# Two DMA queues instead of one for the count stage of a graph network kernel

## The reference

```python
# block 1: attention, 12 heads of 64 features, one weight per head shared
ft = einsum('nhd,ed->nhe', hh, W_fc); a1 = (ft*attn_l).sum; a2 = (ft*attn_r).sum
e = leaky_relu(a1[src] + a2[dst]); alpha = softmax of e over the edges of each dst
x = layernorm(x + relu(hh @ W_res + segment_sum(alpha * ft[src], dst)))
# block 2: three RGCN layers, 3 relations, mean over the edges of a relation
agg = sum over edges of (h @ w_rel[type])[src] / count[dst, type]
h = relu(agg + h @ w_root + bias)
x = layernorm(x + h)
```

## Time and profile before

| | value |
|---|---|
| time, median of three runs | 2580.96 us |
| time of the profiled execution | 2578.14 us |
| span of the profiled execution | 2576.2 us |
| mean granted TensorE clock | 0.929 of full speed |
| PE busy | 2263.1 us, 88% of the span |
| DVE busy | 1224.7 us, 48% |
| ACT busy | 781.5 us, 30% |
| POOL busy | 439.2 us, 17% |
| hardware queue (q1) | 98495 packets, 147.04 MB, 20.4% of 16 engines |

### The profile page before, as it was taken

The page is one execution under the profiler, slowest core; times in us unless marked ns, Lnnn a source line. Parts: engine busy times, 40 slices in busy tenths (PEclk is TensorE's granted clock), DMA queues, the critical chain, the costliest instruction groups (busy, mean ns, idle before and its releaser), DMA issues.

```text
span 2576.2 us, 30017 instructions
## 1 busy us (share of the span) xinstructions
PE 2263.1 (88%) x11025; PEld 1873.5 (73%) x11026; DVE 1224.7 (48%) x1882; ACT 781.5 (30%) x1062; POOL 439.2 (17%) x332
## 2 busy tenths in 40 slices
PE   3997752599999837999999999999999999999997
PEld 1554531143333327999999989999999989999997
DVE  8886646578778435223233243232332343334335
ACT  0132223466767623112121132121221231212212
POOL 0000001578778920000000000000000000000000
PEclk9999875788888968999999999999999999999999
DMA  0133331111001052323343332333333433334332
GB/s 17 50 85 90 88 88 54 55 27 31 28 18 31 15 153 87 93 86 104 114 112 92 95 108 66 110 104 92 101 101 93 117 103 92 109 115 126 105 104 78
DMA packets 137956, 214.80 MB, mean 83 GB/s; under 512 B 86909, under 2 KB 87147, under 8 KB 137830
## 3 DMA queue, kind: packets, MB, share of 16 engines
q1 hardware_dynamic: 98495, 147.04, 20.4%
q0 software_dynamic: 39344, 66.16, 9.1%
HBM read 182.32 MB, written 30.56 MB: 83 GB/s over the span
## 4 chain that ended last, share of the span: by engine, by line
PE 56%; DMA 4%; DVE 2%; ACT 2%; issue 0%; SPq 0%; ACTq 0%; DVEq 0%
PE banks L1072 28%; PE banks L1044 26%; DMA w_raw<-in_L_gnn_w_root_dram 3%; DVE w_lo L1313 1%; ACT w_hi L1192 1%; DMA s_x<-x_tiles 1%; PE banks L1107 0%; PE banks L1081 0%; DMA emb_raw<-in_L_gnn_w_rel_dram 0%; PE banks L1094 0%; PE banks L1125 0%; DVE h_lo L1344 0%; DVE tail_stats L1363 0%; ACT accT L1220 0%; DVE back L1361 0%
## 5 line engine op out<-in xcount | busy, mean ns | idle before, releaser
L1044 PE MATMUL banks<-ct_in,h_hi 125*128 125x416 f32 (+1 forms) x1710 | 604.5, 354 | 0.6 <-ACT accT L1177 0.6
L1044 PE MATMUL banks<-ct_in,h_lo 125*128 125x416 f32 (+1 forms) x1710 | 603.3, 353 | 0.0
L1072 PE MATMUL banks<-g_hi,w_hi 128*128 128x416 f32 (+1 forms) x1440 | 518.5, 360 | 20.6 <-DVE g_lo L1335 20.6
L1072 PE MATMUL banks<-g_lo,w_hi 128*128 128x416 f32 (+1 forms) x1440 | 514.1, 357 | 0.0
L1072 PE MATMUL banks<-g_hi,w_lo 128*128 128x416 f32 (+1 forms) x1440 | 513.7, 357 | 0.0
L1313 DVE TENSOR_TENSOR w_lo<-w_raw,w_hi 128x768 fp32r<-128x768 f32 (+1 forms) x228 | 227.8, 1000 | 470.7 <-ACT w_hi L1192 470.7
L822 PE MATMUL head_sums<-pw,x 125*65 125x512 f32 x720 | 309.8, 583 | 65.5 <-POOL pw L624 46.7
L1192 ACT CAST w_hi<-w_raw 128x768 fp32r<-128x768 f32 (+1 forms) x228 | 197.8, 868 | 453.0 <-PE banks L1072 355.5
L624 POOL TENSOR_TENSOR pw<-y,csum 125x1250 f32<-125x1250 f32 x120 | 314.3, 2648 | 114.8 <-ACT y L669 55.6
L1044 PEld LDWEIGHTS banks<-ct_in,h_lo 125*128 125x128 f32 x1710 | 323.7, 189 | 4.4
L1044 PEld LDWEIGHTS banks<-ct_in,h_hi 125*128 125x128 f32 x1710 | 322.5, 189 | 4.1 <-ACT accT L1177 0.8
(11 more groups left out here) (183 smaller groups left out, 1604.7 us busy)
## 6 DMA issues: line engine op xcount, KB each, us to landing
w_raw<-in_L_gnn_w_rel_dram SPq DMA_DIRECT2D x117, 384.0 KB, 3.2
ct_in<-s_ct POOLq DMA_DIRECT2D x18, 2031.2 KB, 28.6
w_raw<-in_L_gnn_w_rel_dram SPq DMA_DIRECT2D x54, 448.0 KB, 4.3
ct_in<-s_ct POOLq DMA_DIRECT2D x9, 2041.0 KB, 28.1
s_ct<-ct_stage SPq DMA_DIRECT2D x30, 610.4 KB
w_raw<-in_L_gnn_w_root_dram SPq DMA_DIRECT2D x39, 384.0 KB, 3.4
w_raw<-in_L_gnn_w_root_dram SPq DMA_DIRECT2D x18, 448.0 KB, 6.2
low_spread<-s_low SPq DMA_DIRECT2D x12, 610.4 KB
```

The source lines that it names most:

```text
L1044: ins = nc.tensor.matmul(pb[0:rows, PA, 0:s.w], a, b, start=j == 0, stop=j == len(pairs) - 1)
L1072: ins = nc.tensor.matmul(pb[:, m, 0:s.w], a, b, start=s.first and j == 0, stop=s.last and j == len(parts) - 1)
```

## The change

The load of the next x tile, the third count matrix and the degree row are issued by ScalarE in place of SP. SP keeps the residual and the first two count matrices. The x load stands at the head of `keep_turned`, behind its wait for `xt_turned` and ahead of the wait and copy to `xT`. The other two stand at the end of ScalarE's `tile`, ahead of `no_edges`, behind a wait for the tile's own five windows. The loop on SP runs over all tiles, since its last one no longer differs.

```diff
+        def counts_at(tt, b, r):
+            return dram["ct"][r].rearrange("(s p) (u c d) -> p s u c d", p=T, c=2, d=T)[:, :, bass.ds(tt, 1), b].rearrange(
+                "p s u d -> p s (u d)")
...
-            def tile(tt, b, more=True):
+            def tile(tt, b):
                 g = tt * 2 + b
-                if more:
-                    sp.wait_ge(xt_turned, g + 1)
-                    sp.dma_start(xs[:], io["x"][bass.ds((g + 1) * T, T), :]).then_inc(x_in, 16)
                 sp.wait_ge(proj_kept, g * 5 + 5)
                 sp.dma_start(dram["res"][bass.ds(g * T, T), :], res[:].rearrange("p m f -> p (m f)")).then_inc(proj_out, 16)
                 tile_staged(sp, tt, b)
-                for r in range(R):
-                    sp.dma_start(dram["ct"][r].rearrange("(s p) (u c d) -> p s u c d", p=T, c=2, d=T)[:, :, bass.ds(tt, 1), b].rearrange(
-                        "p s u d -> p s (u d)"), stage[0:T, b, r]).then_inc(stored[b], 16)
-                sp.dma_start(dram["deg"][bass.ds(g, 1), :],
-                             stage[T:T + 1, b].rearrange("a r s d -> a (r s d)")).then_inc(stored[b], 16)
-
-            with sp.Fori(0, NT // 2 - 1) as tt:
+                for r in range(R - 1):
+                    sp.dma_start(counts_at(tt, b, r), stage[0:T, b, r]).then_inc(stored[b], 16)
+
+            with sp.Fori(0, NT // 2) as tt:
                 tile(tt, 0)
                 tile(tt, 1)
-            tile(NT // 2 - 1, 0)
-            tile(NT // 2 - 1, 1, False)
...
             def keep_turned(g):
                 act.wait_ge(xt_turned, g + 1)
+                if not (isinstance(g, int) and g == NT - 1):
+                    act.dma_start(xs[:], io["x"][bass.ds((g + 1) * T, T), :]).then_inc(x_in, 16)
                 act.wait_ge(proj_done, g)
...
                     if i == 2:
                         keep_products(g)
+                tile_staged(act, tt, b)
+                act.dma_start(counts_at(tt, b, R - 1), stage[0:T, b, R - 1]).then_inc(stored[b], 16)
+                act.dma_start(dram["deg"][bass.ds(g, 1), :],
+                              stage[T:T + 1, b].rearrange("a r s d -> a (r s d)")).then_inc(stored[b], 16)
```

## The result

The changed kernel takes 2629.01 us (median of four runs, 2622.49 to 2636.68) against 2579.61 us for the kernel before in the same comparison. The ratio is 1.0192, 95% interval 1.0171 to 1.0213: slower by some 49 us, where 22 to 23 us had been forecast. The direction came true, and so did the main mechanism: an issue on ScalarE is held behind the large one ahead of it. The time lies in the range of 2566 to 2645 us, but the loss is more than twice the one that was forecast.

What follows compares the result with a forecast made beforehand. DMA engines were taken to bound the count stage's second half; ScalarE's held issues put tile 9's last window +31.7 us, the stage's end +22 us (417.2 for 395.1): 2600, as median 2603 us, range 2590 to 2613, 8 of 10 within 2566 to 2645.

Steps and rivals of the forecast that it cites:

- The stream stays at the engines' limit: Count stage: two queues move no fewer bytes; stream stays at 165 packets per us, 28.7 to 30.0 us a tile.
- About five of the 16 engines: Count stage: 125-partition transfers use and fill about five of 16 DMA engines, 127 GB/s.
- What an issue costs: End of each tile on ScalarE: degree row held behind the third matrix, bounds 4.7 and 9.9 us, 8.7 taken.
- From `nbr` to xT: Start of each tile: after the csum and `nbr` copies, turning x until the xT copy takes 0.9 us.
- nothing on the path: x load's issue on ScalarE, ahead of a copy wanted only after window 1, costs no time.
- the gaps: Time from the previous tile's last window to the xT copy: 12.3 us for each of tiles 2 to 9.
- The own stretch kept from before: Each tile's time from xT copy to its own last window stays as before; middle 19.3 us for three late tiles.
- The tail: End of count stage: stores after tile 9's last window take 0.85 + 22.7 + 0.85 us, ending at 417.2.
- Rival 1: ScalarE's issues: one descriptor generator for both issuers lengthens the degree row's hold to 16.4 us; 2665 us; chance 0.18.
- Rival 2: Count stage: second queue brings bandwidth of its own, -15 to -45 us, middle -25, 2556 us; chance 0.17.
- Rival 3: Count stage: same engines, ScalarE stall about 5 us or none; -9 to +5 us, 2579 us; chance 0.19.

Runs made afterwards that it cites:

- SP stands back: Changed kernel, but SP issues its two matrices only after ScalarE's csum copy; 2599.83 us, 1.0082.
- TensorE is kept busy: Changed kernel plus 40 zero matmuls in window 0 of each tile but the first: 2630.79 us; only in tiles 2, 4, 6 and 8: 2633.3 us.
- the kernel before in two pieces: Kernel before, all on SP, each 125-partition transfer of the stage cut into 112 and 13 partitions; 2530.5 us, 0.9811.
- The changed kernel in two pieces: Changed kernel, split over SP and ScalarE kept, with the same cut into 112 and 13 partitions; 2567.86 us, 0.9956.
- the degree row first: Changed kernel with ScalarE's two stores at a tile's end swapped, degree row ahead of the third matrix; 2605.87 us, 1.0105.

## Why the prediction was right in sign and wrong in size

*The stream stays at the engines' limit*: right. It runs at 170 packets per us with two queues; with the shape cut, one queue gave nearly twice that. "About five of the 16 engines" is borne out in so far as rate and share rose only when the 125 was gone; no view counts the engines. The 38% are 6.1 of 16 and more than five engines can be, so that share, which the prediction took as agreement, is not a count of busy engines. By the Trainium skill (DMA: Bandwidth & Descriptors, "Why a DMA increments its semaphore by 16 and not by 1") 125 gives 5 engines and 112 gives 16. The traces agree in direction: 38% of the engines with 125 partitions, 91% with 112 and 13. In the forecast I used the rule only against the change and did not ask what another shape would do.

*What an issue costs*: right in kind, too small in size. The degree row was held 8.1 to 9.9 us, mean 9.4, in tiles 1 to 8; 8.5 to 9.9 had been given and the low end taken. With the waits and gaps around the two issues the csum copy comes 10.2 us behind the window for 8.7: 1.5 us times eight, 12 us.

*From `nbr` to xT*: 0.9 us was assumed. It is 2.0 to 2.1 in seven of eight tiles. TensorE has just stood 8 to 10 us, and the turn takes 1.51 us for 0.86; the granted clock in tile 2's turn is 0.50, that is 1.2 GHz. The x issue, which I had called "nothing on the path", takes 0.3 us ahead of the copy. That is some 1.1 us times eight, 9 us. Together the gaps are 21 us longer than forecast (119.6 for 98.4).

*The own stretch kept from before*: this step failed. "Its own stretch from xT copy to last window I keep from the earlier trace rows" gave 160.2 us; measured 173.3, 13 us more. Nothing in the rows of before showed that this stretch would stay the same once ScalarE is held. Of the 13 us, some 9 lie at one place: in tiles 2 to 9 TensorE starts window 4 after a gap of 1.4 to 2.0 us that the profile lists as "issue", 13.5 us in sum, where it was 0.2 to 0.9 us before, 4.6 in sum. Tile 4 of the changed kernel and tile 4 of the kernel before:

```profile
242.68 0.20 PE L395 MATMUL win<-zero_a 125*128 125x1 bf16 x2 [1.84 <-issue]
```

```profile
208.52 0.20 PE L393 MATMUL win<-zero_a 125*128 125x1 bf16 x2 [0.59 <-issue]
```

The gap stays when SP stands back (0.9 to 2.0 us) and when TensorE is kept busy (1.4 to 2.0 us); in the kernel before in two pieces it is at most 0.6 us. The changed kernel in two pieces has such gaps too, at other windows. The kernel with the third matrix alone on ScalarE rules out the nearest causes. TensorE stands there 8.3 to 11.8 us for x in tiles 5, 7 and 9, as long as in the changed kernel or longer. The turn takes 1.51 us there too, and window 1's multiplications in tile 5 take 4.54 us for 4.70. Here are its turn and its start of window 4 in tile 5:

```profile
225.36 1.51 PE L428 MATMUL tp<-ident,x_tile 125*128 125x125 f32 x6 [8.32 <-DMA x_tile<-in_x_dram]
243.02 0.20 PE L398 MATMUL win<-zero_a 125*128 125x1 bf16 x2 [0.31 <-issue]
```

Window 4's gap is 0.2 to 0.3 us in these three tiles, and their own stretches sum to 60.5 us, for 58.9 before and 64.0 in the changed kernel. So neither the long stand nor the low clock after it makes the gap by itself. By runs, the own stretches sum to 157 to 160 us with x alone, with the matrix alone and with the degree row on SP. They are 170 to 175 us in the changed kernel, with the degree row first and with SP standing back, where an issue holds ScalarE in all of these tiles or all but the last. With the degree row on SP the gap is 1.4 to 1.6 us in the four tiles where x is held 6.3 us or more, and at most 0.3 us in those where it is held 4.0 to 4.4. What in a held ScalarE makes the gap stays open, and so does the rest of the 13 us.

*The tail*: right. 451.6 less the last window at 426.5 is 25.1 us; 24.4 were forecast. So 12 + 9 + 13 + 1 = 35 us, less 0.6 us by which tile 1 ended earlier, is the miss at the end of the stage (451.6 for 417.2), and 5 us of it came back in attention.

*Rival 1* (one generator, lock wait): not seen. The first matrix's issue on ScalarE took 0.28 us though SP's began in the same moment (210.84), and with x alone on ScalarE its issue passed in 0.27 us in the midst of a held issue of SP's; under the lock that the rival assumed it would have waited there. The Trainium skill (Perfetto Trace Analysis, "DMA Instruction — HWDGE (DVE, Sync)") states a generator that is shared and locked for exclusive use; no lock wait shows in these rows. *Rival 2* (bandwidth of its own): out, by the packet rate, 170 per us. *Rival 3* (stall of 5 us): such a stall came only where SP was made to stand back, and even there the ratio was 1.0082: by the table the gaps are 16 us and the own stretches 15 us longer than before.

## What to carry to other kernels

A DMA queue that looks full may be a few full DMA engines: put bytes per time and share of the engines side by side before adding a queue, and compare with a transfer of another partition count. Here cutting 125 partitions into 112 and 13 was worth 48 us and a second queue cost 49. Here an issue was cheap only with nothing large ahead of it on its queue, and the one behind a large one was held, whatever it was. So keep issues that can stand behind a large one off an engine that others wait for, and count each unheld issue there at 0.3 to 1.1 us times the tiles. A stretch of work that another engine paces is not a constant to be carried over from the trace of before: here it grew by 13 us.

## What the runs showed of the hardware that was not expected

- The hold of an issue moves to the next issue on that queue: degree row 8.1 to 9.9 us (changed kernel), x load 6.3 to 8.1 us in tiles 2 to 8 (degree row first), degree row 4.5 to 5.0 us with the engines for its queue alone.
- With 16 engines about 90% busy, stores in 500-byte packets ran at 220 to 272 GB/s for some 2 us and then at about 160; the changed kernel in two pieces fell to the same level with two queues.
- Issues of 112- and 13-partition stores took 1.1 to 1.8 us for the pair on ScalarE without a long hold, against 0.28 us for the single 125-partition store.
